# A two-layer transformer block: the expert stage's last three slices by token halves, with the layer norm moved in beside them

## The chip, the cores and the metric

One core of a Trainium2 chip runs the whole kernel. Times are device microseconds of that core; the kernel is launched once per time. Shown with the kernel are the times of its runs and one profiled execution.

## The reference

The input is x, 32 batches of 32 tokens of 256 values (1024 tokens), and a condition vector per batch. Cut to what matters:

```
x = x + layer0(conv(x, cond))        # rmsnorm, 16-head attention, then 8 experts, top 2, 176 wide
x = x + layer1(x, cond)              # layer norm modulated by cond, 16-head attention, MLP, low-rank experts

# end of layer 0
eg, eu = tok @ wg.T, tok @ wu.T              # all experts: 8*176 = 1408 hidden values
moe    = combine-weighted sum of (silu(eg) * eu) @ wd
hidden = hidden + moe
# start of layer 1
ln  = (x - mean) / sqrt(var + 1e-6)
x1  = ln * (1 + scale1) + shift1             # scale1, shift1 per batch
qkv = x1 @ qkv_w + qkv_b                     # q, k, v: 16 heads of 128
```

## The kernel before, in words

Each engine has its own instruction list, written out by hand in the order in which it runs; engines wait for each other with counting semaphores. There is no planner: the order in the functions is the order on the engine.

Every large product is done in float32 accuracy with three matmuls: each operand is split in a high part and a low part, and hi*hi, hi*lo and lo*hi are added in PSUM (`split_mm`, lines 1288 to 1290). ScalarE makes a high part (a rounding copy), GpSimd or VectorE the low part (a subtraction).

**Expert stage.** The 1408 hidden values are 11 slices of 128 (`MI`), the tokens two halves of 512 (`CHUNKS`), so there are 22 units (m, c), in the order of the list `MOE`. For unit n TensorE does `moe_up(n)`, 12 matmuls of 512 columns, into two PSUM banks (gate and up); ScalarE takes silu of the gate (`gate(n)`, line 704); VectorE multiplies by the up half (line 1087) and by the combine weights (`weigh`, line 1076); ScalarE makes the high part (`hidden_hi`, line 698, issued after `gate(n + 1)`), VectorE the low part (line 1079); TensorE does `moe_down(n)`, 12 matmuls of 256 columns, which accumulate in PSUM banks 0 and 1 for the first token half and 2 and 3 for the second. `moe_down(n - 2)` follows `moe_up(n)`. Before the change only the last two slices, 9 and 10, are taken by halves: (9, 0), (10, 0), (9, 1), (10, 1).

The weights of a slice pass through three slots (`SS`). SyncE loads slice m after unit 2(m - 2) - 1 was weighed (lines 422 to 426); ScalarE makes the high parts (`moe_slice_hi`, lines 599 and 605) after the products of slice m - 3, which had the slot, were done; GpSimd makes the low parts (lines 485 and 527). ScalarE does it for slice n/2 + 1 at unit n.

**Layer norm.** Tokens are 8 tiles of 128. VectorE adds the experts' sum from PSUM to the residual, two tiles at a time (`residual1`, lines 1100 and 1101), takes mean and variance (1105, 1106); GpSimd makes the inverse root (473, 474); VectorE normalizes (`ln_apply`, 1109); TensorE transposes the tile and the residual's tile (`turn_z`, lines 1513 and 1515); ScalarE copies the latter (`take_x1`, 729); VectorE modulates the former from PSUM (1119, 1121); ScalarE makes its high part (`mod_hi`, 734) and GpSimd its low part (`mod_lo`, 540). Tiles 0 to 3 go through this between the last `moe_down` and the first projection. Tiles 4 to 7 go beside the projections of unit 0, at the places `Z_BEHIND`.

**Attention of layer 1.** There are 8 units u: 4 groups of 4 heads by 2 token halves. `proj1(u)` makes 12 PSUM banks of 512 columns, in the order q (4 heads), k (4 heads), v (4 token tiles); ScalarE copies each out of one of two alternating banks (lines 754 and 759). Then come the scores (`scores1`), the softmax, `pv1` and the output product. The products for q and k need the whole token half, that of v needs one tile.

Between the stages ScalarE also splits weight pieces 4 and 5 (`piece_hi`, line 592), which unit u = 2 is the first to use, and SyncE loads pieces 8 and 9 after that.

## Time and profile before

| | |
|---|---|
| median of 3 runs | 686.26 us (685.34 to 691.87) |
| profiled execution | 689.74 us, span 688.0 us |
| TensorE busy (PE) | 611.8 us, 89% |
| VectorE busy (DVE) | 398.7 us, 58% |
| ScalarE busy (ACT) | 330.3 us, 48% |
| GpSimd busy (POOL) | 184.2 us, 27% |
| mean granted TensorE clock | 0.928 of 2.4 GHz |

Busy times are of the profiled execution and its span. The expert stage runs from about 240 to 344 us, layer 1's attention from 356 us on. In a timeline a row is one instruction or several like ones; where the idle time before it is over a small bound, it stands in brackets with what ended it. PE durations are modelled ends; the distance from one matmul's start to the next is what it costs.

### The profile page before, as it was taken

The page shows a single profiled execution, that of the slowest core. Times are in us where ns is not written, and L with a number is a line of the kernel's source. Part 1 is how long each engine was busy: PE and PEld are TensorE (multiplying, and loading weights), DVE is VectorE, ACT ScalarE, POOL GpSimd, SP SyncE. Part 2 cuts the span into 40 slices and gives each one's busy share as a digit, 9 for nine tenths or more (in the row PEclk, how much of TensorE's full clock was granted, in tenths as well). Part 3 has the DMA queues.
Part 4 walks back from the last instruction along what each step waited for, and adds up shares of the span by engine and source line. Part 5 has one row for each costly group of instructions (what it writes and reads, how often), then busy time and mean ns, then how long its engine had stood idle before and what let it go on. Part 6 is the DMA issues. An engine that isn't in the chain of part 4 may idle for free.

```text
span 688.0 us, 13799 instructions
## 1 busy us (share of the span) xinstructions
PE 611.8 (89%) x5664; PEld 508.7 (74%) x5664; DVE 398.7 (58%) x748; ACT 330.3 (48%) x852; POOL 184.2 (27%) x192
## 2 busy tenths in 40 slices
PE   4399999999995889999959999999999998589997
PEld 2278777787774768888838888888888886368776
DVE  3589778777787456875482462352433527852553
ACT  2495666756774035533235554454444343365440
POOL 1525433243432122543042240121112003532000
PEclk8578999999997789999969999999999998699989
DMA  9350000000000344445100211101000002101013
GB/s 269 104 247 2 1 1 2 3 2 1 1 2 1 98 154 140 138 138 168 62 0 1 63 56 39 31 23 43 0 2 1 2 1 62 31 1 30 1 63 123
DMA packets 12607, 36.30 MB, mean 53 GB/s; under 512 B 2152, under 2 KB 3688, under 8 KB 11936
## 3 DMA queue, kind: packets, MB, share of 16 engines
q1 hardware_dynamic: 12544, 35.41, 15.9%
q8 instruction: 45, 0.74, 0.4%
q14 instruction: 18, 0.15, 0.1%
HBM read 34.29 MB, written 1.11 MB: 51 GB/s over the span
## 4 chain that ended last, share of the span: by engine, by line
PE 78%; ACT 7%; DVE 6%; issue 4%; DMA 2%; POOL 1%; SPq 1%; DVEq 0%; ACTq 0%
PE ps L1288 18%; PE ps L1289 17%; PE ps L1290 17%; PE ps L1401 9%; PE ps L1561 4%; PE ps L1358 2%; PE ps L1712 2%; ACT raw_s L659 2%; PE ps L1386 2%; DMA work<-in_cols 1%; PE ps L1372 1%; PE ps L1549 1%; ACT work L652 1%; PE ps L1433 1%; ACT hid L617 1%
## 5 line engine op out<-in xcount | busy, mean ns | idle before, releaser
L1155 DVE SCALAR_TENSOR_TENSOR strm_lo<-ps,col,strm_hi 128x512 fp32r<-128x512 f32 x32 | 24.0, 751 | 115.5 <-ACT strm_hi L770 114.4
L478 POOL TENSOR_TENSOR w_lo<-raw_w,w_hi 128x1024 fp32r<-128x1024 f32 x18 | 45.4, 2538 | 125.5 <-ACT w_hi L592 110.8
L1288 PE MATMUL ps<-act_hi,w_hi 128*128 128x512 f32 x160 | 65.2, 407 | 5.6 <-POOL act_lo L540 3.3
L1401 PE MATMUL ps<-raw_w,raw_s 128*128 128x256 f32 x256 | 63.6, 395 | 6.4 <-ACT raw_s L659 6.4
L754 ACT ACTIVATE work<-ps,col 128x512 f32<-128x512 f32 x64 | 44.2, 690 | 51.3 <-PE ps L1290 51.2
L1288 PE MATMUL ps<-w_hi,act_hi 128*128 128x512 f32 x160 | 65.3, 408 | 1.9 <-DVE act_lo L905 1.5
L1289 PE MATMUL ps<-act_lo,w_hi 128*128 128x512 f32 x160 | 64.1, 401 | 0.0
L1290 PE MATMUL ps<-act_hi,w_lo 128*128 128x512 f32 x160 | 63.9, 400 | 0.0
L1289 PE MATMUL ps<-w_lo,act_hi 128*128 128x512 f32 x160 | 63.2, 395 | 0.0
L1290 PE MATMUL ps<-w_hi,act_lo 128*128 128x512 f32 x160 | 63.1, 394 | 0.0
L1401 PEld LDWEIGHTS ps<-raw_w,raw_s 128*128 128x128 f32 x256 | 48.1, 197 | 15.4 <-ACT raw_s L659 9.7
L1288 PE MATMUL ps<-act_hi,strm_hi 128*128 128x512 f32 x104 | 43.2, 416 | 2.6 <-POOL w_lo L527 1.7
L585 ACT ACTIVATE junk<-ps 128x128 f32<-128x128 f32 x160 | 43.9, 339 | 0.0
L1288 PE MATMUL ps<-w_hi 128*128 128x256 f32 (+1 forms) x120 | 38.2, 318 | 5.8 <-DVE w_lo L1079 4.7
L1289 PE MATMUL ps<-act_lo,strm_hi 128*128 128x512 f32 x104 | 42.4, 407 | 0.0
L1290 PE MATMUL ps<-act_hi,strm_lo 128*128 128x512 f32 x104 | 42.2, 406 | 0.0
L1288 PEld LDWEIGHTS ps<-act_hi,w_hi 128*128 128x128 f32 x160 | 31.1, 194 | 13.2 <-issue 5.4
L1079 DVE TENSOR_TENSOR w_lo<-work,w_hi 128x512 fp32r<-128x512 f32 x22 | 23.5, 1066 | 29.5 <-ACT w_hi L698 29.5
L585 ACT ACTIVATION_READ_ACCUMULATOR junk<-ps 128x1 f32 x160 | 40.4, 272 | 0.0
L652 ACT ACTIVATE work<-ps 128x512 f32<-128x512 f32 x40 | 23.8, 617 | 31.3 <-PE ps L1358 31.3
L1561 PEld LDWEIGHTS ps<-bd,work 128*128 128x128 f32 x256 | 33.9, 200 | 5.3 <-issue 3.4
L1290 PE MATMUL ps<-w_hi,w_lo 128*128 128x256 f32 (+1 forms) x120 | 37.9, 316 | 0.0
(183 smaller groups left out, 1446.2 us busy)
## 6 DMA issues: line engine op xcount, KB each, us to landing
raw_w<-in_w_attn SPq DMA_DIRECT2D x16, 512.0 KB, 4.6
raw_s<-in_w_moe SPq DMA_DIRECT2D x11, 384.0 KB, 4.4
work<-comb_dram SPq DMA_DIRECT2D x10, 256.0 KB, 3.9
work<-comb_dram SPq DMA_DIRECT2D x18, 128.0 KB, 2.9
raw_w<-in_w_qkv SPq DMA_DIRECT2D x4, 512.0 KB, 10.7
raw_w<-in_w_o SPq DMA_DIRECT2D x1, 2048.0 KB, 9.9
raw_s<-in_w_ffn SPq DMA_DIRECT2D x8, 256.0 KB, 2.6
bd<-in_w_ada SPq DMA_DIRECT2D x1, 1536.0 KB, 6.4
```

Source lines behind the costliest of these rows:

```text
L478: G.tensor_tensor(flat(w_lo[:, slot]), raw, flat(f32(w_hi[:, slot])), ALU.subtract).then_inc(s_piece_lo, 1)
L585: A(junk[:, squares[0] % 3, 0:n], src, ACT.Square, accum_out=total).then_inc(s_squares, 1)
L652: A(qkT[:, k * BANK:(k + 1) * BANK], ps[:, QK_BANK[k], :], ACT.Copy).then_inc(s_qkT_copied, 1)
L659: A(attnT4[:, :, b, :], ps[:, 4 + b, :].rearrange("p (h q) -> p h q", h=HQ), ACT.Copy).then_inc(s_pv0_copied, 1)
L754: A(dst[:, h * BANK:(h + 1) * BANK], src, ACT.Identity, bias=c_(b, 4 * j + h)).then_inc(s_q1_copied, 1)
L1079: V.tensor_tensor(hid_lo[:, n % 2, :], hm[:, n % 3, :], f32(hid_hi[:, n % 2, :]), ALU.subtract).then_inc(s_hm_ready, 1)
L1155: V.scalar_tensor_tensor(flat(strm_lo[:, n % SS]), ps[:, 4 + n % 2, :], c_("bv", 4 * (u // CHUNKS) + h), flat(f32(strm_hi[:, n % SS])), AL ...
L1288: mm(dst, ah, bh, start=start and i == 0, stop=False, **flags)
L1289: mm(dst, ah, bl, start=False, stop=False, **flags)
L1290: last = mm(dst, al, bh, start=False, stop=stop and i == len(terms) - 1, **flags)
L1401: mm(ps[:, 7, 0:D], attnT[:, h * P:(h + 1) * P], wo0[:, h, :], start=(h == 0), stop=(h == HQ - 1)).then_inc(s_o0_head, 1)
L1561: last = mm(ps[:, 4 + n % 2, t * P:(t + 1) * P], v1[:, u % 2, t, h * DH:(h + 1) * DH], bd[:, u % 2, 4 * h + t].rearrange("p b q -> p (b q) ...
```

## The change

The list `MOE` now ends with three slices by token halves: (8, 0), (9, 0), (10, 0), (8, 1), (9, 1), (10, 1). The first half's sum is then complete at unit 18, three units before the end.

- TensorE's order is written out at the end: `moe_up(16)`, `moe_down(14)`, `moe_down(15)`, `moe_up(17)`, `moe_down(16)`, `moe_up(18)`, `moe_down(17)`, `moe_up(19)`, `moe_down(18)`, `moe_up(20)`, `moe_up(21)`, `turn_z(0)`, `moe_down(19)`, `turn_z(1)`, `moe_down(20)`, `turn_z(2)`, `moe_down(21)`, `turn_z(3)`.
- ScalarE takes slices 9 and 10 at units 15 and 16 instead of 16 and 18.
- VectorE's order puts the steps of the first half's norm between the last units: `residual1(0)`, `stats1(0)`, unit 20, `residual1(1)`, `stats1(1)`, `apply1(0)`, unit 21, and then the rest.
- `turn_z` for tiles 0 to 3 writes PSUM banks 0 and 1, which `residual1` has freed. The residual's transposes are a function of their own, `turn_x1`, with its own semaphore, and run inside unit 0's projections. The buffer `z` moves to another place in `work`.
- In units 0 and 1 the v projections come first (`V_FIRST`), each waiting for its own tile; the first four banks of unit 0 are 4 and 5. `scores1` of these units waits for all 12 copies.
- ScalarE's `piece_hi` of pieces 4 and 5 moves behind unit 0's copies; `mod_hi(2)` and `mod_hi(3)` stand among the copies of unit 0's v.
- Tiles 4 to 7 are transposed ahead of projections 6, 8, 10 and 11 instead of 4, 6, 8 and 10.

```diff
--- before.py
+++ after.py
@@ -158,7 +158,7 @@
         v1_ = work[:, 8 * BANK:16 * BANK]
         v1 = v1_.rearrange("p (r t n) -> p r t n", r=2, t=CT)
         zx = work[:, 16 * BANK:16 * BANK + 6 * D]
-        z = zx[:, 0:2 * D].rearrange("p (r n) -> p r n", r=2)
+        z = zx[:, 4 * D:6 * D].rearrange("p (r n) -> p r n", r=2)
         mt = zx[:, 2 * D:4 * D].rearrange("p (r n) -> p r n", r=2)
         mt2 = zx[:, 0:4 * D].rearrange("p (r n) -> p r n", r=4)
         x2s = qT1.rearrange("p (t n) -> p t n", t=TILES)
@@ -265,6 +265,7 @@
         s_sg_ready = sem("sg_ready")
         s_moe_u = sem("moe_u")
         s_zT = sem("zT")
+        s_x1T = sem("x1T")
         s_xT1_copied = sem("xT1_copied")
         s_s1 = sem("s1")
         s_q1_copied = sem("q1_copied")
@@ -330,9 +331,20 @@
         NL = CHUNKS * MR
         HD = DH // 2
 
-        MOE = [(m, c) for m in range(MI - 2) for c in range(CHUNKS)] + [
-            (MI - 2, 0), (MI - 1, 0), (MI - 2, 1), (MI - 1, 1)]
-        Z_BEHIND = (4, 6, 8, 10)
+        MOE = [(m, c) for m in range(MI - SS) for c in range(CHUNKS)] + [
+            (m, c) for c in range(CHUNKS) for m in range(MI - SS, MI)]
+        LAST0 = NM - SS - 1
+        V_FIRST = (8, 9, 10, 11, 0, 1, 2, 3, 4, 5, 6, 7)
+        Z_BEHIND = (6, 8, 10, 11)
+
+        def order1(u):
+            return V_FIRST if u < CHUNKS else range(12)
+
+        def proj1_bank(n):
+            return 4 + n % 2 if n < CT else n % 2
+
+        def z_bank(t):
+            return t % 2 if t < CT else 4 + t % 2
 
         FFN = ([(m, c) for c in range(CHUNKS) for m in range(SS)]
                + [(m, c) for m in range(SS, MM - SS) for c in range(CHUNKS)]
@@ -714,7 +726,13 @@
                 if n >= 1:
                     hidden_hi(n - 1)
                 f = n // CHUNKS + 1
-                if n % CHUNKS == 0 and SS <= f < MI:
+                if n == NM - 2 * SS - 1:
+                    f = MI - 2
+                elif n == NM - 2 * SS:
+                    f = MI - 1
+                elif n % CHUNKS or f > MI - SS:
+                    f = 0
+                if f >= SS:
                     act.wait_ge(s_hm_used, CHUNKS * (f - SS + 1))
                     moe_slice_hi(f)
                 i = n // CHUNKS - 1
@@ -724,7 +742,7 @@
 
 
             def take_x1(t):
-                act.wait_ge(s_zT, t + 1)
+                act.wait_ge(s_x1T, t + 1)
                 src = ps[:, 6 + t % 2, 0:D].rearrange("p (m n) -> p m n", m=DK)
                 A(xT[:, :, t * P:(t + 1) * P], src, ACT.Copy).then_inc(s_xT1_copied, 1)
 
@@ -736,16 +754,20 @@
 
             def take_proj1(u):
                 j = u // CHUNKS
-                for k in range(12):
-                    if u == 0 and k in Z_BEHIND:
-
-                        t = CT + Z_BEHIND.index(k)
+                for i, k in enumerate(order1(u)):
+                    if u == 0 and i < CT:
+                        if i >= 2:
+                            mod_hi(i, i, mt[:, i % 2, :])
+                        take_x1(i)
+                    if u == 0 and i in Z_BEHIND:
+
+                        t = CT + Z_BEHIND.index(i)
                         take_x1(t)
                         if t > CT:
                             mod_hi(t - 1, t - 1, mt[:, (t - 1) % 2, :])
-                    n = 12 * u + k
+                    n = 12 * u + i
                     act.wait_ge(s_proj1, n + 1)
-                    src = ps[:, n % 2, :]
+                    src = ps[:, proj1_bank(n), :]
                     if k < 8:
                         if k == 0 and u >= 1:
                             act.wait_ge(s_s1, u)
@@ -759,6 +781,9 @@
                         A(v1[:, u % 2, k - 8, :], src, ACT.Copy).then_inc(s_q1_copied, 1)
                 if u == 0:
                     mod_hi(TILES - 1, TILES - 1, mt[:, 1, :])
+                    act.wait_ge(s_hm_used, NM)
+                    for i in range(RAWS, WSLOTS):
+                        piece_hi(NPROJ + i, i % RAWS, i)
 
             def take_pv1(u, heads):
                 for h in heads:
@@ -770,14 +795,8 @@
                     A(flat(strm_hi[:, n % SS]), ps[:, 4 + n % 2, :], ACT.Identity,
                       bias=c_("bv", 4 * (u // CHUNKS) + h)).then_inc(s_pv1_hi, 1)
 
-            act.wait_ge(s_hm_used, NM)
-            for i in range(RAWS, WSLOTS):
-                piece_hi(NPROJ + i, i % RAWS, i)
-            for t in range(CT + 1):
-                if t < CT:
-                    take_x1(t)
-                if t >= 1:
-                    mod_hi(t - 1, t - 1, mt[:, (t - 1) % 2, :])
+            for t in range(2):
+                mod_hi(t, t, mt[:, t % 2, :])
             for u in range(U + 1):
                 if u < U:
                     take_proj1(u)
@@ -1079,23 +1098,26 @@
                 V.tensor_tensor(hid_lo[:, n % 2, :], hm[:, n % 3, :], f32(hid_hi[:, n % 2, :]),
                                 ALU.subtract).then_inc(s_hm_ready, 1)
 
-            for n in range(NM):
+            def hidden(n):
                 dve.wait_ge(s_sg_ready, n + 1)
                 dve.wait_ge(s_moe_u, n + 1)
                 if n >= 2:
                     dve.wait_ge(s_hm32, n - 1)
                 V.tensor_tensor(hu[:, n % 2, :], sg[:, n % 2, :], ps[:, 5 + 2 * (n % 2), :], ALU.mult).then_inc(s_hu_ready, 1)
 
-                if n == 1:
-                    weigh(0)
-                if n >= 1:
-                    weigh(n)
+            hidden(0)
+            hidden(1)
+            weigh(0)
+            weigh(1)
+            for n in range(2, LAST0 + 2):
+                hidden(n)
+                weigh(n)
             dve.wait_ge(ld_xtok, 16)
 
             def residual1(a):
 
                 c = 2 * a // CT
-                dve.wait_ge(s_hm_used, NM - CHUNKS * (CHUNKS - 1 - c))
+                dve.wait_ge(s_hm_used, NM - SS * (CHUNKS - 1 - c))
                 t2 = slice(2 * a, 2 * a + 2)
                 link(V.tensor_tensor(hid[:, t2, :], ps[:, a, :].rearrange("p (b n) -> p b n", b=2), hid[:, t2, :], ALU.add))
                 V.tensor_tensor(xres[:, t2, :], xres[:, t2, :], hid[:, t2, :], ALU.add).then_inc(s_x1_ready, 1)
@@ -1120,25 +1142,44 @@
                                      over(ada[:, scale * DK:(scale + 1) * DK, b4], SEQ), ALU.mult))
                 V.tensor_tensor(m4, m4, over(ada[:, shift * DK:(shift + 1) * DK, b4], SEQ), ALU.add).then_inc(s_mod, 1)
 
-            def ln1(tiles):
-                a = tiles[0]
-                for t in range(a, a + CT + 2):
-                    if t < a + CT:
-                        if t % 2 == 0:
-                            residual1(t // 2)
-                        dve.wait_ge(s_x1_ready, t // 2 + 1)
-                        ln_stats(xres[:, t, :], t, s_lnst)
-                    if a + 1 <= t <= a + CT:
-                        dve.wait_ge(s_lrstd, t)
-                        if t >= 3:
-                            dve.wait_ge(s_zT, t - 2)
-                        ln_apply(z[:, (t - 1) % 2, :], xres[:, t - 1, :], t - 1, 32, s_z_ready)
-                    if t >= a + 2:
-                        dve.wait_ge(s_zT, t - 1)
-                        modulate(ps[:, 4 + t % 2, 0:D], t - 2, t - 2, mt[:, t % 2, :], 2, 1, 0, s_xn1_ready)
-
-            ln1(range(0, CT))
-            ln1(range(CT, TILES))
+            def stats1(t):
+                dve.wait_ge(s_x1_ready, t // 2 + 1)
+                ln_stats(xres[:, t, :], t, s_lnst)
+
+            def apply1(t):
+                dve.wait_ge(s_lrstd, t + 1)
+                if t >= 2:
+                    dve.wait_ge(s_zT, t - 1)
+                ln_apply(z[:, t % 2, :], xres[:, t, :], t, 32, s_z_ready)
+
+            def mod1(t):
+                dve.wait_ge(s_zT, t + 1)
+                modulate(ps[:, z_bank(t), 0:D], t, t, mt[:, t % 2, :], 2, 1, 0, s_xn1_ready)
+
+            residual1(0)
+            stats1(0)
+            hidden(NM - 2)
+            weigh(NM - 2)
+            residual1(1)
+            stats1(1)
+            apply1(0)
+            hidden(NM - 1)
+            weigh(NM - 1)
+            for t in range(2, CT + 2):
+                if t < CT:
+                    stats1(t)
+                if t - 1 < CT:
+                    apply1(t - 1)
+                mod1(t - 2)
+            for t in range(CT, TILES + 2):
+                if t < TILES:
+                    if t % 2 == 0:
+                        residual1(t // 2)
+                    stats1(t)
+                if CT <= t - 1 < TILES:
+                    apply1(t - 1)
+                if t - 2 >= CT:
+                    mod1(t - 2)
 
 
             def softmax1_head(u):
@@ -1487,9 +1528,8 @@
                 last.then_inc(s_hm_used, 1)
 
             pe.wait_ge(s_hid_attn, TILES)
-            for n in range(NM + 2):
-                if n < NM:
-                    moe_up(n)
+            for n in range(LAST0 - 2):
+                moe_up(n)
                 if n == 1:
 
                     pe.wait_ge(s_comb, 1)
@@ -1503,27 +1543,59 @@
                 if n >= 3:
                     moe_down(n - 2)
 
+            moe_up(LAST0 - 2)
+            moe_down(LAST0 - 4)
+            moe_down(LAST0 - 3)
+            moe_up(LAST0 - 1)
+            moe_down(LAST0 - 2)
+            moe_up(LAST0)
+            moe_down(LAST0 - 1)
+            moe_up(LAST0 + 1)
+            moe_down(LAST0)
+
 
             def turn_z(t):
                 pe.wait_ge(s_z_ready, t + 1)
                 if t >= 2:
                     pe.wait_ge(s_mod, t - 1)
+                if t < CT:
+                    pe.wait_ge(s_x1_ready, t % 2 + 1)
+                elif t < CT + 2:
+                    pe.wait_ge(s_q1_copied, CT)
+                for m in range(DK):
+                    last = nc.tensor.transpose(ps[:, z_bank(t), m * P:(m + 1) * P], z[:, t % 2, m * P:(m + 1) * P], ident)
+                last.then_inc(s_zT, 1)
+
+            def turn_x1(t):
+                pe.wait_ge(s_x1_ready, t // 2 + 1)
+                if t >= 2:
                     pe.wait_ge(s_xT1_copied, t - 1)
                 for m in range(DK):
-                    nc.tensor.transpose(ps[:, 4 + t % 2, m * P:(m + 1) * P], z[:, t % 2, m * P:(m + 1) * P], ident)
-                for m in range(DK):
                     last = nc.tensor.transpose(ps[:, 6 + t % 2, m * P:(m + 1) * P], xres[:, t, m * P:(m + 1) * P], ident)
-                last.then_inc(s_zT, 1)
+                last.then_inc(s_x1T, 1)
+
+            moe_up(NM - 2)
+            moe_up(NM - 1)
+            turn_z(0)
+            moe_down(NM - 3)
+            turn_z(1)
+            moe_down(NM - 2)
+            turn_z(2)
+            moe_down(NM - 1)
+            turn_z(3)
 
             def proj1(u):
                 j, c = divmod(u, CHUNKS)
                 s = slice(c * BANK, (c + 1) * BANK)
-                pe.wait_ge(s_xn1_ready, CT * (c + 1))
-                for k in range(12):
-                    if u == 0 and k in Z_BEHIND:
-                        turn_z(CT + Z_BEHIND.index(k))
-                    n = 12 * u + k
+                for p, k in enumerate(order1(u)):
+                    if u == 0 and p < CT:
+                        turn_x1(p)
+                    if u == 0 and p in Z_BEHIND:
+                        turn_z(CT + Z_BEHIND.index(p))
+                        turn_x1(CT + Z_BEHIND.index(p))
+                    n = 12 * u + p
                     i = 4 * j + k // 4
+                    pe.wait_ge(s_xn1_ready, CT * c + (k - 7 if k >= 8 else CT))
                     w = i % WSLOTS
                     if k % 4 == 0:
                         pe.wait_ge(s_piece_lo, NLO + i + 1)
@@ -1535,10 +1607,10 @@
                     else:
                         t = tokens(c * CT + k - 8)
                         terms = [(act_hi[:, m, t], act_lo[:, m, t], w_hi[:, w, m, :], w_lo[:, w, m, :]) for m in range(DK)]
-                    split_mm(ps[:, n % 2, :], terms).then_inc(s_proj1, 1)
+                    split_mm(ps[:, proj1_bank(n), :], terms).then_inc(s_proj1, 1)
 
             def scores1(u):
-                pe.wait_ge(s_q1_copied, 12 * u + 8)
+                pe.wait_ge(s_q1_copied, 12 * u + (12 if u < CHUNKS else 8))
                 if u >= 1:
                     pe.wait_ge(s_s1_shifted, u)
                 for h in range(4):
@@ -1607,10 +1679,6 @@
                         last = nc.tensor.transpose(ps[:, bank, m * P:(m + 1) * P], z2[:, t, m * P:(m + 1) * P], ident)
                     last.then_inc(s_z2T, 1)
 
-            pe.wait_ge(s_x1_ready, 1)
-            for t in range(CT):
-                turn_z(t)
-            pe.wait_ge(s_x1_ready, 2)
             for u in range(U + 1):
                 if u < U:
                     proj1(u)
```

## Rows read from the trace of the kernel before

**Rows 1.** the page's first part, busy us by engine

```profile
PE 611.8 (89%) x5664; PEld 508.7 (74%) x5664; DVE 398.7 (58%) x748; ACT 330.3 (48%) x852; POOL 184.2 (27%) x192
```

**Rows 2.** busy time by stretch: stretch, length, engines, granted clock, DMA share, GB/s

```profile
316.36:344.40 28.04, 25.89 (x157) 22.82 (x155) 15.62 (x22) 7.82 (x15) 4.84 (x4) 1.00 0.34 109
344.40:356.32 11.92, 3.98 (x18) 2.60 (x17) 9.99 (x24) 4.87 (x10) 5.91 (x12) 0.63 0.00 0
356.32:376.95 20.63, 20.63 (x89) 16.61 (x89) 8.83 (x23) 9.32 (x18) 5.21 (x11) 0.88 0.00 1
```

**Rows 3.** TensorE's timeline, start and duration in us, idle time before and its end

```profile
313.61 0.40 PE L1288 MATMUL ps<-act_hi,strm_hi 128*128 128x512 f32 x1
...
316.36 0.28 PE L1288 MATMUL ps<-w_hi 128*128 128x256 f32 x1
...
317.79 0.40 PE L1288 MATMUL ps<-act_hi,strm_hi 128*128 128x512 f32 x1
...
328.04 0.50 PE L1288 MATMUL ps<-act_hi,strm_hi 128*128 128x512 f32 x1 [1.73 <-POOL w_lo L527]
...
342.71 0.39 PE L1288 MATMUL ps<-w_hi 128*128 128x256 f32 x1 [0.42 <-DVE w_lo L1079]
...
356.32 0.77 PE L1288 MATMUL ps<-act_hi,w_hi 128*128 128x512 f32 x1 [2.31 <-issue]
...
361.36 0.39 PE L1288 MATMUL ps<-act_hi,w_hi 128*128 128x512 f32 x1
...
378.81 0.50 PE L1288 MATMUL ps<-act_hi,w_hi 128*128 128x512 f32 x1 [0.57 <-POOL act_lo L540]
```

**Rows 4.** SyncE's timeline of 317 to 319, and the DMA issues of 316 to 325

```profile
318.20 0.58 SPq L426 DMA_DIRECT2D raw_s<-in_w_moe  x1
...
raw_s<-in_w_moe SPq DMA_DIRECT2D x1, 384.0 KB, 4.6
```

**Rows 5.** ScalarE's timeline, last expert units

```profile
323.56 0.60 ACT L704 ACTIVATE work<-ps 128x512 f32<-128x512 f32 x1 [3.06 <-PE ps L1290]
324.05 0.62 ACT L698 ACTIVATE w_hi<-work 128x512 fp32r<-128x512 f32 x1
324.57 0.63 ACT L599 ACTIVATE strm_hi<-raw_s 128x512 fp32r<-128x512 f32 x1
...
344.44 2.00 ACT L592 ACTIVATE w_hi<-raw_w 128x1024 fp32r<-128x1024 f32 x2 [2.51 <-PE ps L1290]
...
351.48 0.41 ACT L734 ACTIVATE act_hi<-work 128x256 fp32r<-128x256 f32 x1
```

**Rows 6.** VectorE's timeline, last expert units and first layer norm

```profile
324.71 0.69 DVE L1079 TENSOR_TENSOR w_lo<-work,w_hi 128x512 fp32r<-128x512 f32 x1 [2.16 <-ACT w_hi L698]
...
326.03 1.37 DVE L1076 TENSOR_TENSOR work<-work 128x512 f32<-128x512 f32 x1
...
343.29 0.69 DVE L1101 TENSOR_TENSOR xres<-xres,hid 128x512 f32<-128x512 f32 x1
344.01 0.43 DVE L1105 BATCH_NORM_STATS2 bst<-xres 128x6 f32<-128x256 f32 x1
...
345.61 0.41 DVE L1109 TENSOR_SCALAR work<-xres,bst,stat 128x256 f32<-128x256 f32 x1 [0.43 <-POOL stat L474]
```

**Rows 7.** GpSimd's timeline, the last slice's split and a norm's low part

```profile
325.58 1.27 POOL L485 TENSOR_TENSOR strm_lo<-raw_s,strm_hi 128x512 fp32r<-128x512 f32 x1 [5.92 <-ACT w_hi L605]
...
350.30 0.73 POOL L540 TENSOR_TENSOR act_lo<-work,act_hi 128x256 fp32r<-128x256 f32 x1 [1.30 <-ACT act_hi L734]
```

**Rows 8.** TensorE's timeline after two long waits, and the stretches beside them

```profile
259.26 0.55 PE L1288 MATMUL ps<-w_hi 128*128 128x256 f32 x1 [4.32 <-DVE w_lo L1079]
...
573.32 0.98 PE L1561 MATMUL ps<-bd,work 128*128 128x128 f32 x3 [2.99 <-issue]
...
258.70:262.10 3.40, 2.84 (x13) 2.87 (x14) 2.67 (x5) 1.29 (x3) 0.00 (x0) 0.50 0.42 117
572.70:579.50 6.80, 6.18 (x22) 5.57 (x23) 4.19 (x7) 1.68 (x3) 1.27 (x1) 0.50 0.36 112
```

## The prediction

> **What bounds the kernel now.** I read the page's totals first, then a table by stretches, then the timelines of the engines around the hand-off from the expert stage to the second layer's attention. TensorE is busy 611.8 of 688.0 us [rows 1], so time goes only where it stands or runs slowly. In the table by stretches [rows 2] the reader is to see one hole: from 344.40 to 356.32 TensorE is booked for 3.98 of 11.92 us, at a mean granted clock of 0.63 (1.2 GHz for most of it), and the next stretch still has 0.88. Before it the clock is 1.00. In TensorE's timeline [rows 3] one `moe_up` (12 matmuls of 512 columns) takes 316.36 - 313.61 = 2.75 us and one `moe_down` 317.79 - 316.36 = 1.43. It waits 1.73 us for slice 10's low part at 328.04, then from 344.40 for the layer norm, and the first projections need 361.36 - 356.32 = 5.04 us for 12 matmuls that take 2.75 at 2.4 GHz.
>
> So at most this can be gained here: 11.92 us, less 1.8 for the 16 transposes that must still run (0.11 each at 2.4 GHz, an estimate from the 0.23 us between matmuls of 512 columns: a quarter, doubled for what is fixed), is 10.1; plus 2.3 for the slow first matmuls. That is 12.4 us, 1.8% of the time.
>
> **Slice 10's load.** Before, `moe_up(19)` is the first unit of slice 10, now it is `moe_up(18)`, and only `moe_up(17)` and `moe_down(16)` stand between the last unit of slice 7 and it. The load doesn't move: SyncE issues it when `weigh(15)` is done, at 318.20, and such a transfer took 4.6 us to land [rows 4], so 322.8. ScalarE now takes the slice right behind `hidden_hi(15)`, before `gate(17)`. It is in order: `gate(17)`, ready at about 320.8, stands behind a wait that ends at 322.8. From rows of ScalarE [rows 5]: slice parts from 322.8 to 323.8, the gate then, `hidden_hi(16)` 0.49 later (324.3), VectorE's low part 0.66 after that (324.95) and 0.69 long, a little more with GpSimd's slice split beside it, as the weighting at 326.03 took 1.37 [rows 6]: 325.7. `moe_down(16)` needs it. `moe_down(15)` ends at 319.22 and `moe_up(17)` at 321.97, so TensorE stands 3.8 us. The old 1.73 goes, since GpSimd's split, from 325.58 to 328.04 before [rows 3, 7], now starts at 323.85 and is over at 326.3. Net +2.1 us.
>
> Bounds: if the transfer lands before 320.8, nothing stands before `moe_down(16)` but the lag of the next paragraph, -3.1; if it takes 2 us more, +2.
>
> **Products one unit behind instead of two.** From here `moe_down(n-1)` follows `moe_up(n)`. Gate matmuls, `gate(n)`, `hidden_hi(n-1)`, low part: before, `moe_up(18)` begins at 321.97 (317.79 for `moe_up(17)`, plus 2.75 and 1.43 [rows 3]), its gate is taken at 323.56, the copy at 324.05, the low part runs 324.71 to 325.40 [rows 5, 6]. That is 3.43 us from the start, and the unit has only 2.75: each product stands 0.75. It happens twice (`moe_down(17)`, `moe_down(18)`): +1.5. Before, only the last product stood so, 0.42, which goes [rows 3]: +1.1 net. `moe_down(18)` then ends at 337.2, 3 us later than the same work before.
>
> **The hand-off.** Now `turn_z(0)` stands ahead of `moe_down(19)` on TensorE's queue. What it waits for is a chain on VectorE, in order. `moe_up(20)` starts at 337.2; the low part of unit 19 ends 3.43 later and its successor starts at 340.6. `residual1(0)` is two instructions of 0.72 (343.29 to 344.01 is one), `stats1(0)` 0.56 with its short second instruction [rows 6]: 342.6. `hidden(20)` and the weighting are of the same size, 0.7 each: 344.0. ScalarE's copy 0.66, low part 0.6: 345.3. `residual1(1)` and `stats1(1)` 2.0: 347.3, `apply1(0)` 0.41 and 0.15 to TensorE: 347.8. TensorE had finished `moe_up(21)` at 337.2 + 2 x 2.75 = 342.7: it stands **5.1 us**, though three products could run. Then `moe_down(19)`, at 349.5; `hidden_hi(21)` waits for exactly that count, so the low part of 21 ends at 351.05, then `stats1(2)` and `apply1(1)`: `turn_z(1)` at 352.0, another 2.5 us. The other two transposes and products follow without a wait, until 355.7.
>
> The v projections have a second chain. `mod_hi(2)` stands on ScalarE behind the copy of v's second bank, and `mod_hi(3)` behind the third: after a product (0.2 to its copy) the copy 0.6, as the gate of the same size, `mod_hi` 0.41 [rows 5], GpSimd's low part 0.73 [rows 7], and short hand-overs. Twice TensorE stands, 1.8 and 1.7 us. The sum of new waits is 5.1 + 2.5 + 3.5 = +11.1; the old hole goes, -10.1 - 2.3. Net -1.3. Bounds: -12.4, if nothing of the chain shows; and +3, if the norm of tile 3 too is late.
>
> **Around the scores.** In unit 0 the last copies are now those of k, which `scores1(0)` needs: about 0.9 us (product to copy 0.2, copy 0.69) where v's products covered it. The wait of 0.57 before unit 1's first projection [rows 3] goes, since v needs only tile 4. In unit 1 `pv1(0)` covers the same thing. ScalarE's two copies of pieces 4 and 5, 2.00 us [rows 5], lay in the hole; now they stand ahead of the first exponential and unit 1's copies. TensorE has two banks, 2.7 us of products, ahead of the first copy it needs, so between 0 and 2.0 shows; I take 0.8. Net +1.1. SyncE's queue has only loads of pieces 8 and 9 behind these, needed two units later: nothing. Norms of tiles 4 to 7 keep three projections between each step and the next: nothing, and 1 us if that cover is gone.
>
> **Clock.** First the rows: a wait of 4.32 us that ended at 259.26 has a stretch at 0.50 from 258.70 to 262.10, and one of 2.99 that ended at 573.32 has one from 572.70 to 579.50 [rows 8]. My waits of 3.8 and 5.1 lie among and above these. The first fall costs half of 3.4, 1.7, less 0.5 that slower gates give back to the next wait: +1.2. The second meets a stretch with waits of its own, and two products and the first v's run slowly: +2.3. The Trainium skill (TensorE: Matmul & The Clock Gate, "Loop structure matters more than you think") says that a copy out of PSUM on VectorE doesn't cool TensorE, while a long DMA wait does; by that rule only the first of the two falls, whose wait is for a transfer, and the total would be 2.3 less. The old hole speaks against it: it is all VectorE work and the clock fell in it [rows 2].
>
> **Sum:** 2.1 + 1.1 - 1.3 + 1.1 = +3.0, with the clock +6.5 us. On the profiled execution (689.74, of which 688.0 is the span) that is 696.2; the median of the runs is 686.26, 3.5 lower, so **692.8 us**.
>
> **Rivals.**
> - The clock holds: the wait of 3.8 or 5.1 falls so that no low stretch follows. For it: 1.73 us did nothing. Against: the rows above. +3.0, 689.3 us.
> - Slice 10 comes in time: its transfer lands early enough that ScalarE takes it before `gate(17)` is due. For it: other engines' load is light there; against it: 4.6 us measured. 3.1 and 1.2 less: +2.2, 688.5 us.
> - Faster: `apply1(0)` is ready by the end of `moe_up(21)`. That is the hand-off filled as the order of the code reads; it decides when VectorE reaches the norm 5 us sooner than I find, for instance if ScalarE's copies don't hold the weighting. Then 5.1 + 2.5 + 2.3 go: -3.4, 682.9 us; with slice 10 in time too, -7.7 and 678.6.
> - The clock stays at 1.2 GHz over the whole hand-off, as it did from 347 to 361 before [rows 2, 3]. The three products and four v's cost double, 3 x 1.43 + 4 x 1.37 = 9.8 instead of my 2.3, less what waits absorb, about 4: +10, 696 us. The Trainium skill's same page ("Part 4: PE-mode transpose") says transposes don't count as activity. By that rule the clock waits for products to return, which here stand between them, so this case is the less likely.
>
> **Chances.** Forecast 0.40, clock holds 0.17, slice in time 0.13, faster 0.12, clock low throughout 0.18. The likeliest one's own range is 690 to 695.5. The range takes in the rivals but half of the fast one and the end of the slow one: 683 to 698. This kernel's measurement tells about 1% from no change: 679.4 and 693.1. Below lies only the end of the fast rival, 0.08; above nearly half of the forecast and most of the last rival, 0.36; between, 0.56.
>
> **What would show it.** In the changed profile: a wait of some 4 us just before a `moe_down` with ScalarE's slice copy released by a DMA; waits of 0.7 us before the next two products; a first `turn_z` that waits about 5 us for VectorE's `apply1` and a second 2 to 3 us; waits for GpSimd's `act_lo` before the third and fourth v; a granted clock of 0.5 after the first two. If the first `turn_z` follows `moe_up(21)` at once, the chain on VectorE is wrongly summed and the kernel is faster; if no slice copy waits for a DMA, the first term is wrong.

## The result, and the profile after

The changed kernel takes 697.12 us (median of 5 runs, 692.88 to 698.27), the kernel before 690.59 (5 runs, 685.34 to 691.87): +6.5 us, a ratio of 1.0123, 95% interval 1.0089 to 1.0156. A second measurement (e5) gave 1.0100 (1.0067 to 1.0133). The profiled execution took 692.88, the shortest of its five runs, and its span is 691.1 us, against 689.74 and 688.0 before.

First the timeline of TensorE, changed kernel, answering to [rows 3] (start and duration in us, idle time before and what ended it). Line 1329 is the first matmul of a product of three, 1566 `turn_z`, 1574 `turn_x1`, 1621 the scores, 1633 `pv1`.

```profile
310.26 0.40 PE L1329 MATMUL ps<-act_hi,strm_hi 128*128 128x512 f32 x1
...
317.18 0.28 PE L1329 MATMUL ps<-w_hi 128*128 128x256 f32 x1
...
326.69 0.58 PE L1329 MATMUL ps<-w_hi 128*128 128x256 f32 x1 [3.73 <-DVE w_lo L1098]
...
332.95 0.39 PE L1329 MATMUL ps<-w_hi 128*128 128x256 f32 x1 [0.57 <-DVE w_lo L1098]
...
337.96 0.39 PE L1329 MATMUL ps<-w_hi 128*128 128x256 f32 x1 [0.57 <-DVE w_lo L1098]
...
349.89 0.63 PE L1566 MATMUL ps<-cst,work 128*128 128x128 f32 x2 [4.77 <-DVE work L1131]
...
355.44 0.44 PE L1566 MATMUL ps<-cst,work 128*128 128x128 f32 x2 [2.36 <-DVE work L1131]
...
360.71 0.38 PE L1574 MATMUL ps<-cst,xres 128*128 128x128 f32 x2
...
365.88 0.50 PE L1329 MATMUL ps<-w_hi,act_hi 128*128 128x512 f32 x1 [1.57 <-POOL act_lo L552]
...
369.33 0.50 PE L1329 MATMUL ps<-w_hi,act_hi 128*128 128x512 f32 x1 [1.57 <-POOL act_lo L552]
...
384.65 1.29 PE L1621 MATMUL ps<-work 128*32 128x32 f32 x128 [0.87 <-ACT work L776]
...
389.27 0.47 PE L1329 MATMUL ps<-w_hi,act_hi 128*128 128x512 f32 x1 [0.38 <-ACT work L781]
...
402.97 1.27 PE L1633 MATMUL ps<-bd,work 128*128 128x128 f32 x10
```

`moe_up(15)` starts at 310.26, at 309.43 before, and at 308.28 in the second profile of the changed kernel (e5): executions differ before the change sets in, so lengths are counted from there. Every wait of the prediction is there: 3.73 us before `moe_down(16)`, twice 0.57 before the next products, 4.77 before `turn_z(0)`, 2.36 before `turn_z(1)`, twice 1.57 before v projections, 0.87 before the scores, 0.38 in unit 1. The first `pv1` starts at 402.97, 92.7 us behind `moe_up(15)`; before it was 395.26, 85.8 us behind.

ScalarE and SyncE of the changed kernel, with the DMA issues of 317 to 326, answer to [rows 4, 5] for the first wait:

```profile
316.52 0.62 ACT L710 ACTIVATE w_hi<-work 128x512 fp32r<-128x512 f32 x1
323.81 0.63 ACT L611 ACTIVATE strm_hi<-raw_s 128x512 fp32r<-128x512 f32 x1 [6.67 <-DMA raw_s<-in_w_moe]
...
324.65 0.58 ACT L716 ACTIVATE work<-ps 128x512 f32<-128x512 f32 x1
...
325.13 0.62 ACT L710 ACTIVATE w_hi<-work 128x512 fp32r<-128x512 f32 x1
```

```profile
319.39 0.58 SPq L438 DMA_DIRECT2D raw_s<-in_w_moe  x1
```

```profile
raw_s<-in_w_moe SPq DMA_DIRECT2D x1, 384.0 KB, 4.3
```

Slice 10's load leaves at 319.39 and needs 4.3 us. ScalarE stands 6.67 us until 323.81, when the copy can start, and only then takes the gate (324.65) that had been due at about 321.7, and the high part behind it (325.13).

VectorE of the changed kernel, answering to [rows 6]:

```profile
342.83 0.68 DVE L1122 TENSOR_TENSOR hid<-ps,hid 128x512 f32<-128x512 f32 x1
...
344.28 0.43 DVE L1127 BATCH_NORM_STATS2 bst<-xres 128x6 f32<-128x256 f32 x1
...
345.58 0.69 DVE L1095 TENSOR_TENSOR work<-work 128x512 f32<-128x512 f32 x1
...
349.45 0.38 DVE L1131 TENSOR_SCALAR work<-xres,bst,stat 128x256 f32<-128x256 f32 x1
...
353.83 0.69 DVE L1098 TENSOR_TENSOR w_lo<-work,w_hi 128x512 fp32r<-128x512 f32 x1 [2.68 <-ACT w_hi L710]
...
355.00 0.38 DVE L1131 TENSOR_SCALAR work<-xres,bst,stat 128x256 f32<-128x256 f32 x1
```

`residual1(0)` starts at 342.83, the statistics at 344.28, unit 20's weighting at 345.58, and `apply1(0)` only at 349.45: TensorE's 4.77 us. `apply1(1)` follows at 355.00, behind unit 21's low part (353.83), which had waited for `moe_down(19)`.

The clock, changed kernel, by stretches (length, busy time of TensorE, its weight loads, VectorE, ScalarE, GpSimd, granted clock), answering to [rows 8]:

```profile
326.30:329.70 3.40, 3.01 (x13) 2.97 (x14) 1.63 (x3) 0.00 (x0) 0.93 (x1) 0.53 0.34 117
350.20:353.60 3.40, 2.88 (x14) 2.58 (x12) 0.92 (x2) 0.43 (x1) 0.31 (x1) 0.53 0.01 2
353.60:357.00 3.40, 1.56 (x13) 1.57 (x14) 3.06 (x9) 0.62 (x2) 1.10 (x3) 0.97 0.00 0
357.00:360.40 3.40, 3.36 (x17) 3.07 (x17) 2.85 (x6) 0.42 (x1) 1.90 (x4) 0.52 0.00 0
```

Three stretches ran at about half clock, with TensorE busy for 3.01, 2.88 and 3.36 us; half of that, 4.6 us, is my estimate of what they cost. The kernel before had one such stretch, whose cost by the same estimate is half of 8.13, 4.1 us:

```profile
347.45:361.10 13.65, 8.13 (x23) 5.95 (x24) 11.66 (x27) 3.17 (x8) 6.10 (x13) 0.50 0.00 0
```

**Why the two profiles differ by 3.1 us and the medians by 6.5.** TensorE of the kernel before at `moe_up(15)`, the first `pv1` and the last unit's `pv1`, then of the changed one at the last, each with the busy time from there to the end:

```profile
309.43 0.40 PE L1288 MATMUL ps<-act_hi,strm_hi 128*128 128x512 f32 x1
...
395.26 1.95 PE L1561 MATMUL ps<-bd,work 128*128 128x128 f32 x16
...
573.32 0.98 PE L1561 MATMUL ps<-bd,work 128*128 128x128 f32 x3 [2.99 <-issue]
```

```profile
573.32:688.00 114.68, 98.86 (x432) 79.38 (x432) 59.32 (x138) 44.00 (x78) 22.28 (x33) 0.88 0.13 43
```

```profile
580.97 0.80 PE L1633 MATMUL ps<-bd,work 128*128 128x128 f32 x5 [2.98 <-issue]
```

```profile
580.97:691.10 110.13, 93.86 (x432) 75.41 (x432) 59.09 (x138) 44.02 (x78) 22.25 (x33) 0.94 0.14 44
```

From `moe_up(15)` to this `pv1` it was 573.32 - 309.43 = 263.9 us before, and 580.97 - 310.26 = 270.7 after: +6.8, and all of it lies ahead of the first `pv1` (85.8 and 92.7 us). The rest is the same 432 matmuls, in 114.7 and 110.1 us: the clock was 0.88 in one execution and 0.94 in the other, in a part that the change doesn't touch. Over all 13 profiles of this document this part took 110.1 to 114.7 us. One pair of profiles says +3.1; the loss at the hand-off is +6.8.

### The profile page after: what moved, and what is told of

Its sections match the earlier page's. It is cut to its first block, busy times and chain, and to the rows that moved or that the text cites. A ratio compares the mean times of both kernels' runs of the same rounds, so it can differ in the third digit from the quotient of the medians.

```text
span 691.1 us, 13877 instructions
## 1 busy us (share of the span) xinstructions
PE 608.8 (88%) x5664; PEld 506.6 (73%) x5664; DVE 393.5 (57%) x748; ACT 329.7 (48%) x852; POOL 184.7 (27%) x192
## 4 chain that ended last, share of the span: by engine, by line
PE 76%; DVE 8%; ACT 7%; issue 4%; DMA 3%; POOL 1%; SPq 1%; DVEq 0%; ACTq 0%
PE ps L1329 18%; PE ps L1330 16%; PE ps L1331 16%; PE ps L1442 9%; PE ps L1633 4%; PE ps L1399 2%; PE ps L1780 2%; ACT raw_s L671 2%; PE ps L1427 2%; PE ps L1413 1%; DMA work<-in_cols 1%; PE ps L1621 1%; ACT work L664 1%; PE ps L1474 1%; PE ps L1356 1%
## 5 line engine op out<-in xcount | busy, mean ns | idle before, releaser
L1329 PE MATMUL ps<-w_hi 128*128 128x256 f32 (+1 forms) x120 | 41.0, 341 | 10.5 <-DVE w_lo L1098 9.5
L1098 DVE TENSOR_TENSOR w_lo<-work,w_hi 128x512 fp32r<-128x512 f32 x22 | 21.2, 962 | 40.7 <-ACT w_hi L710 40.7
L1329 PEld LDWEIGHTS ps<-w_hi,act_hi 128*128 128x128 f32 x160 | 30.5, 191 | 14.2 <-issue 3.7
L1331 PE MATMUL ps<-w_hi,w_lo 128*128 128x256 f32 (+1 forms) x120 | 40.0, 333 | 0.0
L1330 PE MATMUL ps<-w_lo,w_hi 128*128 128x256 f32 (+1 forms) x120 | 40.0, 333 | 0.0
## 6 DMA issues: line engine op xcount, KB each, us to landing
raw_w<-in_w_qkv SPq DMA_DIRECT2D x4, 512.0 KB, 10.1
```

Source lines behind the costliest of these rows:

```text
L1098: V.tensor_tensor(hid_lo[:, n % 2, :], hm[:, n % 3, :], f32(hid_hi[:, n % 2, :]), ALU.subtract).then_inc(s_hm_ready, 1)
L1329: mm(dst, ah, bh, start=start and i == 0, stop=False, **flags)
L1330: mm(dst, ah, bl, start=False, stop=False, **flags)
L1331: last = mm(dst, al, bh, start=False, stop=stop and i == len(terms) - 1, **flags)
```

## The experiments

All were timed in 5 rounds beside the kernel before; ratios are to it. Times in one row of the table are of one chip: e1 to e4 shared one, e5 to e8 another, e9 to e11 a third. The changed kernel was timed beside e6 to e8 only (as e5), so what e1 to e4 win over it is given against both of its ratios. The last column is from the profiled execution: us from `moe_up(15)` to the last unit's `pv1`, 263.9 for the kernel before and 270.7 for the changed one. It leaves out the end of the kernel, which differs from execution to execution.

| run | edit | median, us | before, us | ratio, 95% interval | hand-off, us |
|---|---|---|---|---|---|
| e5 | changed kernel again | 694.50 | 687.61 | 1.0100 (1.0067 to 1.0133) | 272.2 |
| e1 | early slice loads | 689.82 | 686.62 | 1.0035 (1.0008 to 1.0061) | 268.1 |
| e2 | high parts first | 691.72 | 686.62 | 1.0065 (1.0047 to 1.0084) | 270.7 |
| e3 | two products ahead of the first transpose | 693.31 | 686.62 | 1.0100 (1.0076 to 1.0124) | 268.7 |
| e4 | e1 + e2 + e3 | 683.34 | 686.62 | 0.9947 (0.9923 to 0.9971) | 259.4 |
| e6 | idle matmuls in the two long waits | 691.64 | 687.61 | 1.0057 (1.0031 to 1.0082) | 268.3 |
| e7 | kernel before with early loads | 687.65 | 687.61 | 0.9992 (0.9967 to 1.0016) | 263.9 |
| e8 | e4 + `apply1(1)` in between | 684.40 | 687.61 | 0.9938 (0.9911 to 0.9965) | 259.5 |
| e9 | kernel before with idle matmuls | 684.29 | 687.45 | 0.9958 (0.9938 to 0.9979) | 260.8 |
| e10 | e8 + first norm in between | 681.04 | 687.45 | 0.9916 (0.9889 to 0.9942) | 257.0 |
| e11 | e8 with q, k first | 687.46 | 687.45 | 0.9991 (0.9973 to 1.0009) | 263.7 |

**e1, the load of slice 10.**

```diff
                 if m >= SS:
+                    sp.wait_ge(s_slice_lo, m - SS + 1)
+                    sp.dma_start(raw_t[:, m % SS, :], w_moe[m])...
                     sp.wait_ge(s_hm_ready, CHUNKS * (m - SS + 1))
                 spread(cb[:, m % SS, :], 0, m, INTER, ld_cb[m % SS])
-                if m >= SS:
-                    sp.wait_ge(s_slice_lo, m - SS + 1)
-                    sp.dma_start(raw_t[:, m % SS, :], w_moe[m])...
```

The edit moves the loads of all slices from slice 3 on, not only that of slice 10.

> The changed kernel with SyncE issuing each expert slice's load before it waits for the combine weights' buffer, instead of behind it. My theory (ScalarE, in order, is held by slice 10's landing, and the gate behind it): the load leaves 6 us or more earlier, the wait of 3.73 us before moe_down(16) shrinks to about 0.6 (the price of one unit's distance), the low-clock stretch after it is gone, and the time is 4 to 5 us less than the changed kernel's 697.1. Rival (the order on ScalarE, slice copy ahead of the gate, costs by itself, whenever the weights land): over 2 us of the wait stay, and less than 2 us are won. Rival two (hand-off waits are refilled later): the wait goes, the time doesn't.

SyncE and TensorE of this kernel:

```profile
307.68 0.42 SPq L435 DMA_DIRECT2D raw_s<-in_w_moe  x1
```

```profile
321.19 0.39 PE L1328 MATMUL ps<-w_hi 128*128 128x256 f32 x1 [0.90 <-DVE w_lo L1097]
...
326.19 0.39 PE L1328 MATMUL ps<-w_hi 128*128 128x256 f32 x1 [0.57 <-DVE w_lo L1097]
```

The load leaves 321.19 - 307.68 = 13.5 us ahead of `moe_down(16)` (7.3 in the changed kernel), and the wait there is 0.90 instead of 3.73. Against the changed kernel's 1.0123 and 1.0100 the ratio is 1.0035: 4.5 to 6 us less. ScalarE no longer waits for a DMA at its slice copy. The load was the cause of this wait; ScalarE's order alone costs 0.3 us more than the 0.57 of its neighbours. The waits account for 2.8 us of the gain. The low stretch behind the first wait is gone too, but the one at the second long wait lasted 10.2 us in this profile; over the hand-off as a whole it was 2.6 and 4.1 us shorter than the two profiles of the changed kernel.

**e2, the v projections.** `mod_hi` of all four tiles ahead of the copies:

```diff
-            for t in range(2):
+            for t in range(CT):
                 mod_hi(t, t, mt[:, t % 2, :])
...
-                        if i >= 2:
-                            mod_hi(i, i, mt[:, i % 2, :])
```

> The changed kernel with ScalarE making all four high parts of the first half's norm before it starts on the projections' copies. My theory: the two waits of 1.57 us before the third and fourth v projection go, and nothing takes their place: 3.1 us less. Rival (GpSimd's low parts or VectorE's modulation are the true limit): the waits move to an earlier projection and the gain is below 1 us.

1.0065, 2.4 to 4 us less, and in its timeline no projection of unit 0 waits. The two waits were ScalarE's order and nothing else. Its profile doesn't show the gain as a whole: the hand-off took 270.7 us, as in the changed kernel, because slice 10's load took 5.7 us to land this time (4.3 there) and the wait for it was longer:

```profile
326.90 0.58 PE L1327 MATMUL ps<-w_hi 128*128 128x256 f32 x1 [5.05 <-DVE w_lo L1096]
```

**e3, the products in the longest wait.**

```diff
-            turn_z(0)
             moe_down(NM - 3)
-            turn_z(1)
             moe_down(NM - 2)
-            turn_z(2)
+            turn_z(0)
+            turn_z(1)
             moe_down(NM - 1)
+            turn_z(2)
             turn_z(3)
```

> The changed kernel with TensorE taking moe_down(19) and moe_down(20) ahead of turn_z(0), and turn_z(0), turn_z(1) ahead of moe_down(21). My theory: VectorE's chain to the first transpose stays as long, but the two products fill 2.9 of the 4.8 us, and unit 21's high part, which waits for moe_down(19), comes 2 us sooner, so the second transpose does too: 3 to 4 us less, and no low-clock stretch at 350. Rival (VectorE's chain alone sets the end of the hand-off, products only move into its waits): less than 1 us.

TensorE of this kernel: `moe_down(20)`, `turn_z(0)`, `turn_z(1)`.

```profile
348.20 0.38 PE L1329 MATMUL ps<-w_hi 128*128 128x256 f32 x1 [1.16 <-DVE w_lo L1098]
...
350.38 0.44 PE L1566 MATMUL ps<-cst,work 128*128 128x128 f32 x2 [0.50 <-DVE work L1131]
353.94 0.50 PE L1566 MATMUL ps<-cst,work 128*128 128x128 f32 x2 [3.12 <-DVE work L1131]
```

The first two waits sum to 1.66 instead of 4.77, but the second transpose waits 3.12 instead of 2.36. The ratio, 1.0100, is within the changed kernel's own intervals: alone it wins 0 to 1.6 us, less than I expected. In TensorE's waits it wins 4.77 + 2.36 - 1.66 - 3.12 = 2.35 us, but in this profile the first wait was 4.91 instead of 3.73 (the load took 5.4 us), and a low stretch still follows the wait of 3.12, which the expectation had ruled out.

**e4, the three together.**

> The three edits together (early slice loads, high parts first, two products ahead of the first transpose). If the three costs are separate, as I think, the gains add: 4.5 + 3.1 + 3.5 = 11 us less than the changed kernel, about 686, some 4 us under the kernel before. If they share one limit (VectorE's chain), the sum stays under 7 us.

0.9947: 10.5 to 12 us under the changed kernel. By the ratios of the first chip, the three alone give 0.0088 + 0.0058 + 0.0023 = 0.0169 of 1.0123, that is 0.9954. Against 1.0100 they would give only 1.0000, so by the ratios the three gains add at least. The waits decide it: those listed for the changed kernel sum to 16.39 us, in e4 to 8.05 (0.90, 0.57, 0.57, 1.15, 0.49, 3.12, 0.87, 0.38), 8.3 less, and e1, e2 and e3 took away 2.83, 3.14 and 2.35, which is 8.3 too. So the three waits were separate. The rest is clock: one low stretch is left, with TensorE busy for 3.4 us.

**e5 and e6, the clock.** e5 is the changed kernel once more.

> The changed kernel as it is, timed once more beside the next three, to have its ratio to the kernel before on the same chip: 1.012 by the first measurement, 1.009 if only waits count (+6 us), 1.004 if the profiled pair (688.0 and 691.1) is typical.

Two stretches of its profile, after the first and during the second long wait and behind it:

```profile
325.93:329.34 3.41, 3.41 (x13) 2.83 (x12) 0.18 (x1) 0.00 (x0) 0.00 (x0) 0.50 0.84 269
346.41:360.06 13.65, 9.37 (x43) 9.07 (x44) 8.73 (x21) 1.46 (x3) 3.79 (x8) 0.50 0.00 1
```

The clock fell in the same places, and this time stayed at half for 13.7 us of the hand-off: half of 3.41 + 9.37 is 6.4 us, where the first profile had 4.6. The waits are the same (16.46 against 16.39 us), and the hand-off took 272.2 us instead of 270.7. The median says +6.9 us. e6 puts matmuls with no use into the waits:

```diff
+            def filler(n, count, used):
+                pe.wait_ge(s_hu_ready, used)
+                for i in range(count):
+                    mm(ps[:, 4, :], strm_hi[:, 0, 0, :], act_hi[:, 0, BANK:2 * BANK], start=True, stop=True)
...
             moe_up(LAST0 - 1)
+            filler(0, 16, 17)
             moe_down(LAST0 - 2)
...
             moe_up(NM - 1)
+            filler(NM - 2, 20, NM - 1)
             turn_z(0)
```

> The changed kernel with 16 idle matmuls of 512 columns ahead of moe_down(16) and 20 ahead of turn_z(0), into a bank that nothing reads: they use nothing but the two long waits (3.7 and 4.6 us). My theory of the clock (each long wait is followed by a stretch at 1.2 GHz, together worth 3.5 us of the +6.5): the granted clock stays at 1.0 from 326 to 360, and the time falls by 2 to 3.5 us. Rival (the waits of VectorE's chain absorb the slow matmuls): the clock stays up and the time moves by less than 1 us.

```profile
318.00:327.00 9.00, 9.00 (x52) 7.72 (x50) 2.38 (x4) 1.94 (x4) 2.65 (x3) 1.00 0.64 219
327.00:349.00 22.00, 20.26 (x103) 16.37 (x103) 12.01 (x22) 4.58 (x8) 1.60 (x4) 1.00 0.15 48
349.00:362.00 13.00, 10.64 (x64) 9.74 (x63) 9.91 (x24) 2.72 (x6) 3.78 (x8) 0.87 0.01 2
```

The clock holds at 1.00 until 349 and falls once, to 0.87 on average, around the wait of 2.36 that was left. 1.0057 against 1.0100 on the same chip: 3.0 us less, though TensorE does 36 matmuls more. The intervals just overlap (1.0031 to 1.0082, 1.0067 to 1.0133), so the size is uncertain, not the clock that the rows show. The hand-off of the profiled execution, 268.3 us, is 2.4 and 3.9 us shorter than in the two profiles without the idle matmuls.

**e7, was the kernel before held by the load?**

> The kernel before with the same early slice loads as in the first experiment. Before, slice 10's copy didn't wait for its load, so only the wait of 1.73 us for GpSimd's split is there, and that hangs on ScalarE's place for it: the time stays within 1 us of the kernel before. Rival (the late load held the kernel before too): 1.5 to 2 us less.

0.9992, and a hand-off of 263.9 us as before: no. The late load cost something only once slice 10 was wanted one unit sooner.

**e8 and e10, VectorE's chain.** Two steps of the norm where VectorE stands for ScalarE's high part anyway:

```diff
-            def weigh(n):
+            def weigh(n, between=None):
...
                                 ALU.mult).then_inc(s_hm32, 1)
+                if between is not None:
+                    between()
                 dve.wait_ge(s_hm_hi, n + 1)
...
-            weigh(NM - 1)
+            weigh(NM - 1, lambda: apply1(1))
...
-                if t - 1 < CT:
+                if 1 < t - 1 < CT:
```

> The three edits of the fourth experiment and, on VectorE, apply1(1) between the weighting of unit 21 and its low part, where VectorE waits for ScalarE. The wait of 3.12 us before turn_z(1) then shrinks to under 1.7, moe_down(21) follows as soon as its low part is there: about 1 us less than that experiment's ratio of 0.9947. If VectorE's later steps set the end, nothing.

TensorE of e8, again `moe_down(20)`, `turn_z(0)` and `turn_z(1)`:

```profile
341.88 0.38 PE L1328 MATMUL ps<-w_hi 128*128 128x256 f32 x1 [1.15 <-DVE w_lo L1097]
...
344.06 0.44 PE L1565 MATMUL ps<-cst,work 128*128 128x128 f32 x2 [0.50 <-DVE work L1130]
345.70 0.44 PE L1565 MATMUL ps<-cst,work 128*128 128x128 f32 x2 [1.21 <-DVE work L1130]
```

The third wait is 1.21 instead of 3.12, but 0.62 and 0.56 stand before the next product and the last transpose. 0.9938 against 0.9947 can't be told apart, and the hand-offs are 259.5 and 259.4 us: the microsecond that I expected wasn't won, the wait went elsewhere.

> The eighth experiment's kernel and, on VectorE, residual1(0) and stats1(0) between the weighting of unit 19 and its low part, where VectorE stands for ScalarE. If VectorE's chain sets the first transposes, as I hold, the waits of 1.15 and 0.50 before moe_down(20) and turn_z(0) shrink and 1 to 1.5 us more are won, a ratio of 0.992. If not, it stays at 0.994.

```diff
-            for n in range(2, LAST0 + 2):
+            for n in range(2, LAST0 + 1):
...
-            residual1(0)
-            stats1(0)
+            def first_norm():
+                residual1(0)
+                stats1(0)
+
+            hidden(LAST0 + 1)
+            weigh(LAST0 + 1, first_norm)
             hidden(NM - 2)
```

Waits of TensorE in e10 from `moe_down(18)` on:

```profile
333.37 0.39 PE L1332 MATMUL ps<-w_hi 128*128 128x256 f32 x1 [0.57 <-DVE w_lo L1097]
...
344.93 0.44 PE L1569 MATMUL ps<-cst,work 128*128 128x128 f32 x2 [1.21 <-DVE work L1130]
345.99 0.58 PE L1332 MATMUL ps<-w_hi 128*128 128x256 f32 x1 [0.62 <-DVE w_lo L1097]
```

No wait is left from `moe_down(18)` at 333.37 to `turn_z(1)` at 344.93. 0.9916: 6.4 us faster than the kernel before by the medians, 5.8 by the ratio, and the fastest here. Against e8 the intervals overlap (0.9889 to 0.9942, 0.9911 to 0.9965); the hand-off is about 2.4 us shorter, of which 1.65 are the two waits.

**e9, what the clock cost the kernel before.** Four to eight matmuls with no use ahead of and behind each `turn_z`, 28 in all.

```diff
+            def filler(count):
+                pe.wait_ge(s_x1_ready, 1)
+                for i in range(count):
+                    mm(ps[:, 0, :], strm_hi[:, 0, 0, :], act_hi[:, 0, BANK:2 * BANK], start=True, stop=True)
...
             for t in range(CT):
+                filler((4, 6, 4, 6)[t])
                 turn_z(t)
+            filler(8)
```

> The kernel before with 28 idle matmuls of 512 columns in its one hole (4, 6, 4 and 6 ahead of the four transposes, 8 behind them), into bank 0, which nothing reads. It tells what the clock alone cost the kernel before: the granted clock stays up from 344 to 361, the first 12 projection matmuls take 2.75 instead of 5.04 us, and the time is 1.5 to 2.5 us less. Rival: the idle matmuls delay the transposes and the clock falls all the same, 0 to 1 us more.

```profile
342.00:360.00 18.00, 15.72 (x78) 11.97 (x79) 15.68 (x37) 6.80 (x13) 7.67 (x17) 1.00 0.00 1
```

The clock is 1.00 where it was 0.63 [rows 2], and the time 2.9 us less (0.9958; the hand-off 3.1), a little more than I had given: in [rows 2] the transposes too were slow, 3.98 us busy where I had counted 1.8. Half of the busy time at low clock had given 4.1 us, so that estimate is rather too high.

**e11, the order of the projections.** `V_FIRST` off, and the scores wait for 8 copies again:

```diff
-            return V_FIRST if u < CHUNKS else range(12)
+            return range(12)
...
-                pe.wait_ge(s_q1_copied, 12 * u + (12 if u < CHUNKS else 8))
+                pe.wait_ge(s_q1_copied, 12 * u + 8)
```

> The eighth experiment's kernel with the projections of units 0 and 1 in the old order, q and k first and v last, to price the change's second part alone. v first lets TensorE start after tile 0 and pays 0.87 us before the scores; q first waits until tile 3's low part is there, 2.3 us later by VectorE's, ScalarE's and GpSimd's steps, and has no wait before the scores: 1 to 1.5 us slower than the eighth experiment, a ratio of 0.996. Rival (the order of the projections is worth nothing): the same 0.994.

TensorE at the first q, the stretch at low clock around it, and the only such stretch of e8's hand-off:

```profile
354.11 0.80 PE L1328 MATMUL ps<-act_hi,w_hi 128*128 128x512 f32 x1 [2.08 <-POOL act_lo L551]
```

```profile
348.30:358.50 10.20, 7.02 (x22) 5.01 (x22) 9.41 (x21) 2.90 (x7) 5.56 (x11) 0.51 0.00 0
```

```profile
346.60:349.90 3.30, 3.14 (x14) 2.92 (x14) 3.16 (x10) 0.42 (x1) 2.17 (x5) 0.50 0.00 0
```

The wait of 2.08 is the one I expected (2.3), but the ratio is 0.9991, 3.6 us slower than e8 (the hand-off about 4): the clock stays low for 10.2 us instead of 3.4, which I had left out; by half the busy time that is 3.5 us against 1.6. So in the repaired kernel v first was worth 3.6 us. What it was worth in the changed kernel itself no run tells; what cost time there were the waits that e1, e2 and e3 removed.

## Why the prediction was right and wrong

It gave +6.5 us and 692.8, with 683 to 698; measured are +6.5 us (697.12 against 690.59) by medians and 1.0123 and 1.0100 by the two ratios, that is 8.5 and 6.9 us. The range holds the time, and every wait stood where it was forecast. Two steps failed.

The first is the last step, **how the numbers follow**: it took 1% as what can be told from no change, gave "between" 0.56 and "above" 0.36. But the 95% intervals of the two ratios reach only 0.0034 and 0.0033 to either side, so the forecast itself, 0.95%, was a loss that would be told. The measured loss, 1.2% and 1.0%, is clear of zero in both intervals; whether it is over or a little under 1% they leave open.

The second is a term of the sum, the **clock**: 3.5 us forecast, 4.6 in the first profile, 6.4 in the second (e5). The account, in us, by the waits listed above and half of TensorE's busy time at low clock:

| | forecast | first profile | e5 |
|---|---|---|---|
| new waits | 18.1 | 16.39 | 16.46 |
| new stretches at low clock | 3.5 | 4.64 | 6.39 |
| old waits and low stretch, gone | -15.1 | -14.73 | -14.73 |
| sum | +6.5 | +6.30 | +8.12 |
| `moe_up(15)` to the last `pv1`, measured | | +6.8 | +8.3 |

The forecast's -15.1 are 1.73, 0.42, 0.57 and the hole's 10.1 and 2.3. Between the sums and the measured lengths 0.5 and 0.2 us stay unexplained. In the first profile the waits, counted 1.7 us too long, hide the clock; in the second they don't, and there the loss is 1.2%. That the medians differ by just the forecast's 6.5 is partly luck. So is the old hole's line: its standing was 7.94 us and not 10.1, its low clock cost 4.07 and not 2.3, and the two errors cancel. Term by term:

- **Slice 10's load**: right, 3.73 us against 3.8; e1 shows the cause. This forecast stood on in-order ScalarE, one issue time and one transfer time. That it came so close is in part the execution: 3.85 in e5, 5.05 and 4.91 in e2 and e3, where the load took 5.7 and 5.4 us.
- **Products one unit behind**: right, 0.57 against 0.75, twice; the rows of the prediction give 3.43 - 2.75 = 0.68 and not 0.75.
- **The hand-off**: right, 4.77 and 2.36 against 5.1 and 2.5, and 1.57 twice against 1.8 and 1.7. These waits were counted 0.8 us too long together.
- **Around the scores**: 0.87 against 0.9, 0.38 against 0.8.
- **Clock**: the mechanism right, the size too small. I gave 1.2 and 2.3; the profile has 1.5 (326.30 to 329.70) and 3.1 (two stretches), by half the busy time: 4.6 against 3.5, and in e5 the second was longer still, 4.7. This is the mis-sized term. It isn't measured in the runs that weren't profiled, but e6, which keeps the clock up at both waits, is 3.0 us faster.
- **The rivals**: that the clock holds is refuted by three rows, that slice 10 comes in time by 323.81. The fast rival, a VectorE that reaches the norm in time, didn't occur; in e10 the first transpose waits for nothing, with the products ahead of it and `residual1(0)` inside the wait for ScalarE. "The clock stays low throughout" is what e5's profile shows over the hand-off, 13.7 us of it, and its loss there, 8.3 us, is less than the +10 I gave.
- **The rule on the clock.** In the changed kernel the wait of 4.77 us was for VectorE and the clock fell at its end (350.20, 0.53), and where idle matmuls filled it (e6) it didn't. The Trainium skill (TensorE: Matmul & The Clock Gate, "Loop structure matters more than you think") says that a copy out of PSUM on VectorE leaves TensorE warm, where the next matmuls follow immediately. The trace agrees for that case: in the first line of [rows 2] VectorE, whose multiplication by the up half reads PSUM, is busy 15.62 us beside dense matmuls, and the clock is 1.00. The wait of 4.77 us, where nothing followed immediately, is another case, and the prediction's "only the first of the two falls" doesn't follow from the page.

Open: why in one execution the clock comes back between 353.6 and 357.0 and in the other not. No run here controls where a stretch begins.

## What to carry to other kernels

Before a unit is moved one place forward, look at who loads for it and how long that load has been on its way: the kernel before had enough lead (e7), the changed one made TensorE stand for 3.73 us, and the repair was to issue the load ahead of another wait on the queue (e1). Interleaving two stages pays only if each engine's own order is written for it: work for the next stage goes where the engine would stand anyway (between a product and the low part that waits for another engine), not ahead of what feeds TensorE; the same change was 1.0 to 1.2% slower as it was written and 0.8% faster with the order of e10. Don't read a change of 1% from one pair of profiles; compare the part that was changed and the part that wasn't.
